# Reordering SyncE's DMA queue in a fused cross-attention and ternary feed-forward kernel: the maxima of group 2, the upper heads' q loads, the output weights

## The reference

```python
x = x + xattn(layernorm(x), ctx, pos)          # 32 heads of 16, rotary positions on q and k
x = x + ffn(layernorm(x))                      # 512 -> 2048 -> 512

def xattn(x, ctx, pos):
    q = rope(x @ Wq, pos); k, v = split(ctx @ Wkv); k = rope(k, pos)
    w = softmax(einsum('bqhd,bkhd->bhqk', q, k) / 4)
    return einsum('bhqk,bkhd->bqhd', w, v) @ Wout + bout

def bitlinear(x, w):                           # twice, with a gelu between them
    xn = layer_norm(x)
    x_hat = clip(xn * 128 / max|xn|) * max|xn| / 128        # per row
    w_hat = sign(round(w / (mean|w| + 1e-6))) * mean|w|     # ternary
    return x_hat @ w_hat.T
```

## Time and profile before

| what | us |
|---|---|
| median of three runs | 761.99 |
| the profiled execution, its own time | 762.23 |
| its span in the trace | 760.4 |
| TensorE matmul busy | 734.2 |
| VectorE busy | 656.8 |
| ScalarE busy | 457.1 |
| GpSimd busy | 432.6 |
| mean granted TensorE clock, of 1 | 0.993 |

### The profile page before, as it was taken

The page is one execution under the profiler, slowest core; times in us unless marked ns, Lnnn a source line. Parts: engine busy times, 40 slices in busy tenths (PEclk is TensorE's granted clock), DMA queues, the critical chain, the costliest instruction groups (busy, mean ns, idle before and its releaser), DMA issues.

```text
span 760.4 us, 11891 instructions
## 1 busy us (share of the span) xinstructions
PE 734.2 (97%) x3886; PEld 313.9 (41%) x3886; DVE 656.8 (86%) x927; ACT 457.1 (60%) x830; POOL 432.6 (57%) x502
## 2 busy tenths in 40 slices
PE   5999999979999999999999999999999999999998
PEld 3787777412222222222222122445555555555443
DVE  6787998878999999989989787379999889998895
ACT  4786766756777777777777688764224432333330
POOL 5787776754555556654555486466474745663310
PEclk9999999989999999999999999999999999999999
DMA  8798998666577778889888785426657665545546
GB/s 278 191 239 231 256 246 195 150 146 181 137 163 169 166 162 167 162 157 182 151 168 172 171 160 117 94 57 137 119 118 125 119 145 117 105 97 105 117 97 139
DMA packets 185715, 118.05 MB, mean 155 GB/s; under 512 B 120068, under 2 KB 150836, under 8 KB 185652
## 3 DMA queue, kind: packets, MB, share of 16 engines
q1 hardware_dynamic: 185654, 117.29, 69.1%
HBM read 64.50 MB, written 25.43 MB: 118 GB/s over the span
## 4 chain that ended last, share of the span: by engine, by line
PE 77%; SPq 7%; DMA 6%; DVE 3%; issue 2%; ACT 2%; POOL 2%; POOLq 0%; DVEq 0%; ACTq 0%
PE banks L1116 15%; PE banks L1101 15%; PE banks L779 12%; PE banks L795 11%; PE banks L310 9%; PE banks L748 6%; PE banks L1082 6%; SPq L658 4%; DMA stack_words<-k_parts 3%; DVE maxima L871 2%; SPq L270 1%; PE banks L341 1%; DMA late_words<-k_parts 1%; SPq L668 1%; PE banks L765 1%
## 5 line engine op out<-in xcount | busy, mean ns | idle before, releaser
L891 ACT ACTIVATE probs_words<-banks 128x512 f32<-128x512 f32 x512 | 266.0, 603 | 85.9 <-PE banks L779 85.7
L871 DVE TENSOR_REDUCE maxima<-banks 128x2 f32<-128x1024 f32 x240 | 278.4, 1214 | 32.6 <-PE banks L748 31.5
L795 PE MATMUL banks<-probs_words,late_words 128*32 128x512 f32 x1024 | 137.8, 611 | 0.4 <-ACT probs_words L891 0.2
L1101 PE MATMUL banks<-ternary_words,late_words 128*128 128x512 f16 x512 | 113.1, 379 | 0.0
L1116 PE MATMUL banks<-ternary_words,stack_words 128*128 128x512 f16 x512 | 112.9, 379 | 0.0
L779 PE MATMUL banks<-stack_words 114*128 114x512 bf16 x352 | 105.1, 390 | 4.1 <-DMA stack_words<-max_rows 3.9
L1300 ACT ACTIVATE probs_words<-probs_words,h_moments 128x2048 f32<-128x2048 f32 (+1 forms) x17 | 32.2, 1902 | 121.3 <-DVE h_moments L1179 121.3
L1101 PEld LDWEIGHTS banks<-ternary_words,late_words 128*128 128x128 f16 x512 | 49.9, 98 | 60.5 <-issue 0.8
L1116 PEld LDWEIGHTS banks<-ternary_words,stack_words 128*128 128x128 f16 x512 | 49.2, 98 | 60.7 <-issue 2.9
L779 PEld LDWEIGHTS banks<-stack_words 114*128 114x128 bf16 x352 | 26.8, 97 | 91.2 <-ACT probs_words L891 71.4
L1294 ACT ACTIVATE probs_words<-banks,row_scale 128x512 f32<-128x512 f32 x64 | 43.0, 685 | 30.7 <-PE banks L1101 30.7
(11 more groups left out here) (162 smaller groups left out, 1129.9 us busy)
## 6 DMA issues: line engine op xcount, KB each, us to landing
o_rows<-late_words SPq DMA_DIRECT2D x32, 256.0 KB, 2.9
k_parts<-ternary_words SPq DMA_DIRECT2D x48, 128.0 KB, 3.4
q_parts<-ternary_words SPq DMA_DIRECT2D x48, 128.0 KB, 2.6
stack_words<-q_parts SPq DMA_DIRECT2D x22, 192.0 KB, 3.1
attn_words<-in_x_dram SPq DMA_DIRECT2D x16, 256.0 KB, 5.0
probs_words<-in_L_ffn_w_fc_dram SPq DMA_DIRECT2D x16, 256.0 KB, 3.5
probs_words<-in_L_ffn_w_proj_dram SPq DMA_DIRECT2D x16, 256.0 KB, 5.3
late_words<-in_L_ffn_w_fc_dram SPq DMA_DIRECT2D x16, 256.0 KB, 3.7
```

The lines of the kernel that those rows point to most:

```text
L795: mm = self.nc.tensor.matmul(self.pv_bank[32 * j:32 * j + 32], self.v_ones[:, g % 2, c, j, :], self.probs[:, c, j, :], start=(c == 0), sto ...
L871: dve.tensor_reduce(self.maxima[:, g % 2].rearrange("p (x i) -> p x i", x=2)[:, :, j], self.score_slot[j % 2], AX.X, ALU.max).then_inc(sel ...
L891: act.activation(self.probs[:, c, head, :], self.st_bank[(g * 16 + k) % self.ST_BANKS], ACT.Exp, scale=1 / math.sqrt(HEAD)).then_inc(self. ...
L1101: mm = self.nc.tensor.matmul(self.fc_bank[o], self.uT[:, n % U_SLOTS, part * KX + k], self.fcT[:, k, o], start=(k + part == 0), stop=(k == ...
```

## The change

All of it is in SyncE's list; no other engine's instructions or order differ. `turn_max(2)` moves ahead of the last twelve part stores, and `load_max(2)` between the sixth and the seventh of them. The weight load of step 2 moves ahead of the wait for all parts. The three q DMAs of the upper heads move from the even step into the odd step before, behind that step's weight load. The four output weights are loaded two at step 26 and two at step 28.

```diff
-    def store_parts(self, sp, n):
+    def store_parts(self, sp, n, which=slice(0, 2 * PARTS)):
...
-        for s, part in ((0, 0), (0, 1), (1, 0), (0, 2), (1, 1), (1, 2)):
+        for s, part in ((0, 0), (0, 1), (1, 0), (0, 2), (1, 1), (1, 2))[which]:
...
-    def load_stacks(self, sp, pair, half):
+    def load_stacks(self, sp, pair, half, both=(0, 1)):
...
-        for t, where, runs in ((0, mem.q_parts, self.Q_RUNS[half]), (1, mem.k_parts, self.K_RUNS[half])):
+        for t in both:
+            where, runs = ((mem.q_parts, self.Q_RUNS[half]), (mem.k_parts, self.K_RUNS[half]))[t]
...
                     att.load_stacks(sp, STACK_PAIRS - 1, 1)
-                if within(s - 5, TILES) and (s - 5) % 2 == 1:
+                    att.turn_max(sp, 2)
+                    prj.store_parts(sp, TILES - 1, slice(0, PARTS))
+                    att.load_max(sp, 2)
+                    prj.store_parts(sp, TILES - 1, slice(PARTS, 2 * PARTS))
+                if within(s - 5, TILES - 1) and (s - 5) % 2 == 1:
                     prj.store_parts(sp, s - 5)
...
                 if s == 2:
+                    att.load_weight(sp, w_fc, w_proj, s)
                     for pair in range(2):
                         sp.wait_ge(prj.parts_stored[pair], PAIR_STORES * BATCH)
-                if s == 3:
-                    att.turn_max(sp, 2)
-                    att.load_max(sp, 2)
                 if 5 <= s < GROUPS + 2:
                     att.turn_max(sp, s - 2)
-                if 2 * STACK_PAIRS <= s + 1 < GROUPS:
-                    att.load_stacks(sp, (s + 1) // 2, (s + 1) % 2)
+                if 2 * STACK_PAIRS <= s + 1 < GROUPS and s % 2 == 1:
+                    att.load_stacks(sp, (s + 1) // 2, 0)
+                if 2 * STACK_PAIRS <= s < GROUPS and s % 2 == 0:
+                    att.load_stacks(sp, s // 2, 1, (1,))
                 if 5 <= s < GROUPS + 2:
                     att.load_max(sp, s - 2)
-                if 2 <= s < GROUPS:
+                if 3 <= s < GROUPS:
                     att.load_weight(sp, w_fc, w_proj, s)
+                if 2 * STACK_PAIRS <= s + 1 < GROUPS and s % 2 == 1:
+                    att.load_stacks(sp, (s + 1) // 2, 1, (0,))
                 att.pack_sums(sp, s)
...
-                if GROUPS - 6 <= s < GROUPS - 2:
-                    rows.load_weight(sp, wout, s - GROUPS + 6)
+                if s in (GROUPS - 6, GROUPS - 4):
+                    for k in range(2):
+                        rows.load_weight(sp, wout, s - GROUPS + 6 + k)
```

## The result

The changed kernel is slower: 766.09 us median of ten runs (764.46 to 769.91) against 761.84 us of ten runs of the kernel before (759.10 to 766.35), ratio 1.0055, 95% interval 1.0032 to 1.0079. That is 2.4 to 6.0 us more, where 4.7 us less had been forecast. The profiled execution of the changed kernel took 769.91 us, the longest of its ten, so its trace shows more of the loss than the median does.

A forecast was written before the change was run, and what follows sets the result against it. TensorE, busy 734 of 760 us, bounds the kernel; only its waits and half clock can be won. Terms +1.2 - 3.3 - 2.9 = -5.0, taken as -4.7 from 762.2, gave 757.4 us; own range 755.5 to 759.2, 8 in 10 754.0 to 761.2.

The forecast's parts named there:

- the two kinds of wait: TensorE's waits on SyncE's queue: one of 3.9 us for a group's maxima, six totalling 4.3 us for k parts.
- The maxima of group 2: Start of step 4: their 3.9 us wait goes, with 2.7 us of half clock behind it.
- The stall comes back at step 5: TensorE waits about 5.1 us for group 3's maxima, half clock behind; the first edit costs about 1.2 us.
- fixed at 13.3 us: Time from the start of ternarise 2 on GpSimd to the landing of group 3's maxima, taken as unchanged.
- 3.1 lost: Latest bound for the start: group 3's maxima land at 181.5 behind the stack loads, losing 3.1 us.
- Its cause: Step 2's weight load, 1.4 us later, delays ternarise 2 on GpSimd and so group 3's maxima.
- The first rival: Start-up stall doesn't come back at step 5: all 6.6 us won, 749 us, or 754 with a wait; chance 0.10.
- The upper heads' q loads, -3.3 us: Even steps: k follows the maxima's transposition 1.50 us earlier, so waits of 0.2 to 1.0 us go, gaining 3.3 us.
- In step 9 the queue stood idle for 1.29 us there, which hides them but for 0.2: Odd steps: idle time ahead of the result store absorbs the moved q loads' 1.50 us but for 0.2.
- Step 28, -2.9 us: Wait of 1.70 us for k parts shrinks to 0.4 with full clock behind it, gaining 2.9 us.
- The row of 5.1 us speaks for the ring: Step 28's k landing 5.1 us after issue: DMAs queued ahead count, not issue alone; otherwise the wait shrinks 0.3 us.
- The slower one: DMA engines' backlog sets k's landing, fuller odd steps delay the rest, k waits stay: 763.2 to 765 us; chance 0.11.

The follow-up runs named there:

- the run with both: Kernel before with step 2's weight load, tile 0's transposition and group 2's maxima ahead of the stores, group 3's maxima earlier: 762.58 against 763.22 us, ratio 0.9982.
- three partial tries: Changed kernel with step 2's weight load first, 766.36 against 764.29 us; the start edit alone, 767.58 against 764.29; the run with both, 762.58 against 763.22.
- q moved, transposition late: Kernel before with upper q loads in the odd step and its weight transposition behind the even step's upper k loads: 759.01 against 764.44 us, ratio 0.9935.
- k ahead of the maxima: Kernel before with even steps ordered upper k, maxima transposition, upper q, weight load, load of maxima: 767.33 against 763.22 us, ratio 1.0051.
- late load of the maxima: Kernel before with upper q loads moved and the even step's load of the maxima behind weight load and sums: 763.21 against 763.22 us, ratio 1.0002.
- k ahead of q: Kernel before with the five upper k DMAs ahead of the three q DMAs at even steps: 763.78 against 763.22 us, ratio 1.0003.

## Why the prediction was wrong

**The views read and the two kinds of wait**: right. Nearly all that moved the attention in the traces, in the change and in the runs, is TensorE waiting for SyncE's DMAs and the clock behind that.

**The maxima of group 2**: the wait goes, as said; transposition at 153.7 (said 153.2), load at 158.92 (158.4).

**The stall comes back at step 5**: right in its mechanism, too small in its size. The weight load went out at 163.60 (said 163.1), GpSimd began at 166.62 (166.0 to 166.6). Then the chain was called fixed at 13.3 us, and it took 14.9: the transposition 6.63 us behind (said 6.66), its load 5.17 us later instead of 4.64, and landing in 3.1 us instead of 2.0. The landing was taken from the load of group 2, which had stood free; the lower-half stack loads in front of this one were named, but kept for the bound. So the wait ended at 181.56 instead of 179.6. The clock was priced right for this trace: step 5 took 194.91 - 181.56 = 13.35 us, said 13.2. Without the 0.7 us that this trace is late ahead of the edit, the start costs 2.6 us instead of 1.2, near the "3.1 lost" of the bounds; the runs of this part alone have medians 3.3 us apart, though its one trace shows only 0.5. The term of the sum that was too small is the landing of one DMA and half a microsecond of issue.

**Its cause**: half right. The load of the weight tile does bind, but it isn't the only one: with it moved ahead, the transposition of tile 0 holds GpSimd until 168.00, and the wait is 6.2 us. The first rival (the stall doesn't come back) couldn't have been had from the load alone, nor from both links, as the run with both shows.

**The upper heads' q loads, -3.3 us**: this is the term that failed; measured, 0. That k goes out directly behind the transposition of the maxima is right. The step that failed reads "In step 9 the queue stood idle for 1.29 us there, which hides them but for 0.2". It took the length of an issue as fixed, and the room of one early step as that of all. Step 9 itself was full in the changed kernel, its q loads taking 2.06 us instead of 1.50; step 15 had 1.43 us of room for 1.34 us of q loads, but its k loads took 1.18 us longer. The maxima of the even groups 8 to 26 then go out up to 2.3 us behind their split, before at most 0.4, and with them the k loads that were to profit. The text had this as "lateness of up to a microsecond" that takes part of the gain; it took the whole.

**Step 28, -2.9 us**: half right at its place. In the changed kernel's trace the splits of groups 27 and 28 end 446.78 - 434.74 = 12.04 us apart, before 13.87, so 1.8 us came, and 0.8 of them went again at step 30. The gain came with the clock, which stayed full, and not with the wait, which is 1.45 instead of the 0.4 that was said; that the clock stays full behind such a wait was not certain, as the last section shows. With the output weights alone its wait is gone and a wait of 2.07 us is at step 30 instead; with the q loads alone step 28 waits 0.45 us and step 30 2.9 us; in the changed kernel both wait 1.45 and 1.47 us. In all three, what was made good at step 28 was lost in part or whole at step 30. The step of it that failed is counting the bytes ahead of k at one step only.

**"The row of 5.1 us speaks for the ring"**: the runs agree that what was queued ahead counts and not the issue alone: the same k loads land in 4.1 or 3.2 us, depending on the transposition ahead. But it was above all the transposition, which the prediction never named among what stood ahead of k. The output weights do count at step 28, where the wait went when they alone were moved; the q parts don't show: the k loads land in 4.0 to 4.1 us with q moved away from in front of them.

**Rivals.** The slower one, which had 0.11, named the place ("in odd steps the fuller queue delays what follows", the k waits stay) and priced it at 763.2 to 765. In its outcome it is what came, at 766.1, 1.1 us above its range. Its reason, a backlog of the DMA engines older than one step, is not shown; the issue and the transposition account for the k waits. Against it was said that the early pairs, with the same bytes, don't wait. That was no evidence that the odd steps have room: in the changed kernel steps 9, 11 and 13 have no gap either and take 11.1 to 11.2 us from mark to mark. TensorE loses nothing by it there, but the queue does: group 13's maxima go out 1.06 us behind their split, before 0.03.

**Open**: how much of the 4.2 us (by the medians) belongs to the start and how much to the full odd step. The start alone is worth 3.3 in its runs and 0.5 in its one trace, the q loads alone nothing in theirs, and in the trace of the changed kernel the waits at groups 14 and 16 cost 5.25 us and the start 2.6. Its wait of 1.99 us at 300.72 with the half clock behind it is something that the trace of the q loads alone has not (0.91 us there, at 296.59); that the two parts make each other worse was not separated.

## What to carry to other kernels

Where one queue carries everything, a DMA moved earlier is paid by whatever follows it there: add up the issue times of the fullest step that receives it before counting the gain, and leave a margin, since the same loads took up to 1.2 us longer to issue here. In a stall that a chain of loads ends, look for all links that end within a microsecond or two of the one named; moving one hands the stall to the next, and only ordering the whole stretch by need collected it (6.2 us, after three partial tries that gave +2.1, +3.3 and -0.6). If a transposing DMA stands just ahead of loads that are awaited and its own result isn't, try it behind them: here that one move gave 3.9 us.

## What the runs showed of the hardware

- Two transposing DMAs in a row ahead of eight loads book the DMA engines at 1.12 to 1.23 over 5 us and the k loads land in 4.1 us; with one moved behind them it is 0.53 to 0.66, at 164 to 181 GB/s either way, and 3.2 us. The landing is not sooner in every such order: with the q loads gone as well, so that k stands directly behind the transposition of the maxima, it is 4.4 and 5.2 us.
- The transposition of the maxima lands in a median of 2.4 us in the kernel before, 4.0 with the q loads alone moved, 3.5 in the changed kernel and 2.6 with the transposition of the weight rows late too.
- A transposing DMA's issue takes 1.1 to 1.7 us of SyncE's queue; a plain one mostly takes 0.34 to 0.71 us.
- TensorE's granted clock was at half behind waits of 1.70 (kernel before), 1.80 (both links moved), 1.88 (q moved, transposition late), 1.99 (changed kernel), 2.07, 2.90 and 3.40 us, and full behind waits of 1.45 and 1.47 (changed kernel), 1.62 and 1.65 us (k ahead of the maxima; late load of the maxima). But it was full too behind 1.75 us (the start alone), 1.82 us (k ahead of q) and 1.80 and 2.23 us (the changed kernel with the weight load first). So the length of the wait alone doesn't decide, and a forecast for a wait between 1.7 and 2.3 us has to allow for both. The wait and a window behind it in that last kernel:

```profile
454.77 0.39 PE L749 MATMUL banks<-stack_words 48*128 48x512 bf16 x2 [2.23 <-DMA stack_words<-k_parts]
```
```profile
456.00:457.00 1.00, 1.00 (x10) 0.16 (x8) 1.00 (x2) 1.00 (x3) 1.00 (x1) 1.00 0.34 60
```

- The step behind a long wait took 13.2 us after one of 3.9 us, 12.2 after one of 5.5 and 13.35 after one of 6.4, against 10.6 of an ordinary one: the same kind of wait costs 1.6 to 2.8 us of clock on top.
- The issue of the same loads isn't of fixed length: in two full odd steps of the changed kernel three k loads took 1.36 us at 218.39 and 2.55 us at 282.82, and in the kernel before 1.36 us at 215.04 and 2.35 us at 321.17.
